# Cross-attention block on one core: inverse roots of the variances on VectorE alone, and the last stage's weights fetched in the last batch

## The reference, cut to what matters

```python
def layer_norm(x, w, b):
    mu = jnp.mean(x, axis=-1, keepdims=True)
    var = jnp.mean(jnp.square(x - mu), axis=-1, keepdims=True)
    return (x - mu) * jax.lax.rsqrt(var + EPS) * w + b

residual = hidden_states
x = layer_norm(hidden_states, ln1_w, ln1_b)
q = x @ q_w + q_b;  k = ctx @ k_w + k_b;  v = ctx @ v_w + v_b      # per head
scores = einsum('bhqd,bhkd->bhqk', q, k) * scale                   # masked
out = einsum('bhqk,bhkd->bhqd', softmax(scores), v)
hidden = out @ cproj_w + cproj_b + residual
y = layer_norm(hidden, ln2_w, ln2_b)
y = gelu(y @ fc_w + fc_b, approximate=True) @ proj_w + proj_b
return hidden + y
```

## Time and profile before

| what | value |
|---|---|
| median of three runs | 750.32 us (749.85 to 750.52) |
| the profiled execution's own time | 747.24 us |
| its span in the trace | 745.4 us |
| TensorE matmuls busy | 698.3 us, 94% of the span |
| ScalarE busy | 457.9 us, 61%; 400.6 of it the 416 exponentials |
| VectorE busy | 370.6 us, 50% |
| GpSimd busy | 122.8 us, 16% |
| mean granted clock of TensorE | 0.981 of full speed |

### The profile page before, as it was taken

How to read it: one execution, slowest core, us unless ns; L and a number is a source line. 1 busy time by engine, 2 the same in 40 slices (tenths; PEclk the granted TensorE clock), 3 DMA queues, 4 the chain that set the end, 5 groups by cost and what they waited for, 6 DMA issues and landing times.

```text
span 745.4 us, 16779 instructions
## 1 busy us (share of the span) xinstructions
PE 698.3 (94%) x7026; PEld 476.8 (64%) x7026; DVE 370.6 (50%) x824; ACT 457.9 (61%) x483; POOL 122.8 (16%) x90
## 2 busy tenths in 40 slices
PE   3679998999999999999999999999998978999997
PEld 3567665666566656665666566656664534697897
DVE  5655663554355535543555355525542322467663
ACT  5406568666865686568656865686566888633311
POOL 6222041003200320041003200410000600011010
PEclk9869999999999999999999999999999999999999
DMA  9677564356544653465346534654435500000000
GB/s 312 185 268 274 185 207 183 136 174 210 189 139 171 210 198 136 165 210 201 137 160 212 199 143 156 211 199 143 160 141 182 187 2 2 1 22 7 30 29 32
DMA packets 51081, 113.76 MB, mean 153 GB/s; under 512 B 6858, under 2 KB 39986, under 8 KB 49722
## 3 DMA queue, kind: packets, MB, share of 16 engines
q1 hardware_dynamic: 40488, 80.56, 31.9%
q10 hardware_dynamic: 10514, 32.08, 11.9%
HBM read 65.30 MB, written 47.06 MB: 151 GB/s over the span
## 4 chain that ended last, share of the span: by engine, by line
PE 77%; ACT 13%; issue 1%; DVE 1%; ACTq 0%; DVEq 0%
PE O L1152 22%; PE S L1145 16%; ACT pr L602 12%; PE XB L1082 11%; PE O L1082 10%; PE O L1239 6%; PE S L1082 6%; PE XB L1179 2%; PE MB L1132 2%; PE XB L1119 2%; PE XB L1111 0%; ACT pj_raw L610 0%; ACT L602 0%; PE O L1132 0%; DVE g_lo L921 0%
## 5 line engine op out<-in xcount | busy, mean ns | idle before, releaser
L602 ACT ACTIVATE pr<-S 128x1024 f32<-128x1024 f32 x416 | 400.6, 1024 | 176.6 <-PE S L1145 172.9
L1152 PE MATMUL O<-pr,vsl 128*17 128x256 f32 x3328 | 224.8, 384 | 1.3 <-DVE ot L816 1.3
L1145 PEld LDWEIGHTS S<-qst,kst 64*128 64x128 f32 x1664 | 116.0, 186 | 117.4 <-ACT pr L602 79.1
L1145 PE MATMUL S<-qst,kst 64*128 64x256 f32 x1664 | 170.5, 313 | 16.9 <-ACT pr L602 13.5
L1152 PEld LDWEIGHTS O<-pr,vsl 128*17 128x17 f32 x3328 | 74.9, 97 | 78.2 <-issue 16.4
L751 DVE TENSOR_SCALAR kpart<-O,cols_s 128x384 fp32r<-128x384 f32 x64 | 40.6, 635 | 120.4 <-PE O L1082 120.4
L526 POOL CAST c_hi<-cT 128x768 fp32r<-128x768 f32 (+1 forms) x28 | 23.9, 852 | 328.4 <-DMA cT<-in_ctx_t 202.9
L797 DVE TENSOR_REDUCE mx<-MB 128x2 fp32r<-128x512 f32 x64 | 44.1, 689 | 64.7 <-PE MB L1132 64.7
L1082 PE MATMUL XB<-w_hi,c_hi 128*128 128x256 f32 (+1 forms) x208 | 68.3, 328 | 2.6 <-DVE vsl L765 1.8
L765 DVE TENSOR_TENSOR vsl<-XB,rows_s 128x256 f32<-128x256 f32 (+1 forms) x104 | 43.3, 416 | 51.0 <-PE XB L1082 51.0
L1082 PE MATMUL O<-c_hi,w_hi 128*128 128x384 f32 (+1 forms) x128 | 52.8, 412 | 17.0 <-POOL c_lo L531 10.5
(11 more groups left out here) (101 smaller groups left out, 842.5 us busy)
## 6 DMA issues: line engine op xcount, KB each, us to landing
kst<-k_scr SPq DMA_DIRECT2D x89, 400.2 KB
k_scr<-kpart SPq DMA_DIRECT2D x48, 384.0 KB, 3.3
v_scr<-vsl ACTq DMA_DIRECT2D x8, 1768.0 KB, 6.0
cT<-in_ctx_t ACTq DMA_DIRECT2D x21, 384.0 KB, 5.0
k_scr<-kpart SPq DMA_DIRECT2D x16, 449.0 KB, 3.3
qst<-q_scr SPq DMA_DIRECT2D x87, 64.0 KB
q_scr<-qpart SPq DMA_DIRECT2D x16, 256.0 KB, 2.5
cT<-in_ctx_t ACTq DMA_DIRECT2D x7, 449.0 KB, 3.5
```

Source lines behind the costliest of these rows:

```text
L602: nc.scalar.activation(pr[:, n % PBUF, :], S[:, 2 * (n % 2):2 * (n % 2) + 2, :] .rearrange("p a n -> p (a n)"), ACT.Exp).then_inc(s_.exp_d ...
L1145: last = nc.tensor.matmul(S[:, 2 * (n % 2) + g_, j * LQ:(j + 1) * LQ], kst[rows_, s, j, kt * P:(kt + 1) * P], qst[rows_, s, j, :], start=T ...
L1152: last = nc.tensor.matmul(O[32 * h:32 * h + VW, 0, 0:LQ], vsl[:, par, s, kt, h * VW:(h + 1) * VW], pr[:, n % PBUF, h * LQ:(h + 1) * LQ], s ...
```

## The change

`newton` becomes `inverse_root`: the first guess comes from the variance's bits, shifted right by one and taken from a constant, and three Newton rounds follow, all on VectorE: eleven instructions, each waiting for the one before. `x_root`, `h_root` and their semaphores go. The five instructions stood at the same places. `load_mlp` moves from step 44 of batch 6 to step 4 of batch 7; its waits are the same. The counts of `ln_steps` and `rstd_steps` follow.

```diff
+ROOT_BITS = 0x5F375A86
+ROUNDS = 3
+NEWTON = 2 + 3 * ROUNDS
...
-            def x_root(t0, t1, steps):
-                act.wait_ge(ln_steps, steps)
-                nc.scalar.activation(rs1[:, 1, t0:t1], rs1[:, 0, t0:t1], ACT.Sqrt).then_inc(ln_root, 1)
-
-            def h_root(s_, i, t0, t1):
-                act.wait_ge(s_.var_done, i + 1)
-                nc.scalar.activation(rs[:, 1, t0:t1], rs[:, 0, t0:t1], ACT.Sqrt).then_inc(s_.root_done, 1)
...
-                    if c == 0 and s_ is first:
-                        h_root(first, 1, HEAD, TOK)
...
-            x_root(0, 2 * QT, XA_VAR)
...
-                    if n == 44 and b + 2 == B:
+                    if n == 4 and b + 1 == B:
                         load_mlp()
-                    if b == 0 and n == 40:
-                        x_root(2 * QT, TOK, XB_VAR)
-                    if b == B - 1 and n == 20:
-                        h_root(first, 0, 0, HEAD)
...
-            def newton(rs_, steps, before, root, roots):
-
-                dve.wait_ge(root, roots)
-                nc.vector.reciprocal(rs_[2], rs_[1]).then_inc(steps, 1)
+            def inverse_root(rs_, steps, before):
+
+                nc.vector.tensor_scalar(rs_[1].bitcast(I32), rs_[0].bitcast(I32), 1, None, ALU.arith_shift_right).then_inc(steps, 1)
                 dve.wait_ge(steps, before + 1)
...
+                nc.vector.tensor_scalar(rs_[2].bitcast(I32), rs_[1].bitcast(I32), -1, ROOT_BITS, ALU.mult, ALU.add
+                                        ).then_inc(steps, 1)
+                for i in range(ROUNDS):
+                    n = before + 2 + 3 * i
+                    dve.wait_ge(steps, n)
+                    nc.vector.scalar_tensor_tensor(out=rs_[3], in0=rs_[2], scalar=-0.5, in1=rs_[2], op0=ALU.mult, op1=ALU.mult
+                                                   ).then_inc(steps, 1)
+                    dve.wait_ge(steps, n + 1)
+                    nc.vector.tensor_tensor(rs_[3], rs_[3], rs_[0], ALU.mult).then_inc(steps, 1)
+                    dve.wait_ge(steps, n + 2)
+                    nc.vector.scalar_tensor_tensor(out=rs_[2], in0=rs_[3], scalar=1.5, in1=rs_[2], op0=ALU.add, op1=ALU.mult
+                                                   ).then_inc(steps, 1)
+                dve.wait_ge(steps, before + NEWTON)
...
                         if s_ is first and c == 1 and i == 0:
-                            newton(rs_rows(rs, HEAD, TOK), first.rstd_steps, TOK + 5, first.root_done, 2)
+                            dve.wait_ge(first.var_done, 2)
+                            inverse_root(rs_rows(rs, HEAD, TOK), first.rstd_steps, TOK + NEWTON)
```

More of the change, by code:

```diff
@@ L277, in build @@
         hi_done, lo_done, kh_done, qh_done, ql_done = map(sem, ("hi_done", "lo_done", "kh_done", "qh_done", "ql_done"))
-        ln_steps, ln_root = sem("ln_steps"), sem("ln_root")
+        ln_steps = sem("ln_steps")
         good_steps, good_ready, flag_done = map(sem, ("good_steps", "good_ready", "flag_done"))
@@ L302, in section @@
             s.var_done = sem(f"{name}_var_done")
-            s.root_done = sem(f"{name}_root_done")
             s.rstd_steps = sem(f"{name}_rstd_steps")
@@ L329, in build @@
         XA_VAR = 4 * QT + 1
-        XB0 = XA_VAR + 5
+        XB0 = XA_VAR + NEWTON
         XB_VAR = XB0 + 2 * (TOK - 2 * QT) + 1
@@ L687, in _ @@
                         exponential(whole, b, n)
-                h_root(whole, 0, 0, TOK)
                 y_t(whole, 0)
@@ L900, in ending @@
                     dve.wait_ge(first.h_steps, ONE + B)
-                    moments(first, HEAD, TOK, HEAD + 5)
+                    moments(first, HEAD, TOK, HEAD + NEWTON)
             def checked():
@@ L958, in _ @@
             head(1)
-            newton(rs_rows(rs1, 0, 2 * QT), ln_steps, XA_VAR, ln_root, 1)
+            dve.wait_ge(ln_steps, XA_VAR)
+            inverse_root(rs_rows(rs1, 0, 2 * QT), ln_steps, XA_VAR)
             k_evac(0, 0, 2)
@@ L1009, in norms @@
                 if b == 0 and p == 24:
-                    newton(rs_rows(rs1, 2 * QT, TOK), ln_steps, XB_VAR, ln_root, 2)
+                    dve.wait_ge(ln_steps, XB_VAR)
+                    inverse_root(rs_rows(rs1, 2 * QT, TOK), ln_steps, XB_VAR)
                 if b == B - 1 and p == 5:
@@ L1014, in norms @@
                 if b == B - 1 and p == 12:
-                    newton(rs_rows(rs, 0, HEAD), first.rstd_steps, HEAD, first.root_done, 1)
+                    dve.wait_ge(first.var_done, 1)
+                    inverse_root(rs_rows(rs, 0, HEAD), first.rstd_steps, HEAD)
                 if b == B - 1 and p == YN_AT:
@@ L1070, in _ @@
                 moments(whole, 0, TOK, 0)
-                newton(rs_rows(rs, 0, TOK), whole.rstd_steps, TOK, whole.root_done, 1)
+                dve.wait_ge(whole.var_done, 1)
+                inverse_root(rs_rows(rs, 0, TOK), whole.rstd_steps, TOK)
                 normalise(whole, 0)
```

8 lines of the change are left out of this document (removed).

## The result

| | before | after |
|---|---|---|
| median, first comparison | 750.09 us (4 runs, 749.58 to 750.52) | 739.14 us (4 runs, 738.16 to 739.85) |
| ratio | | 0.9863 (95%: 0.9837 to 0.9888) |
| median over the later series (the changed kernel with the four above) | 748.85 us (89 runs; 748.87 with the four above) | 739.38 us (14 runs) |
| profiled execution, its span | 747.24, 745.4 us | 738.16, 736.4 us |
| busy: TensorE, ScalarE, VectorE | 698.3, 457.9, 370.6 us | 690.8, 446.9, 379.8 us |

The change makes the kernel 9.5 us faster (748.85 − 739.38). The kernel before also spreads: single executions of it took 745.9 to 755.6 us, so three runs did not give its median to a microsecond.

What follows compares the result with a forecast made beforehand. TensorE, with 77% of the chain, was taken as the bound, waiting on ScalarE's exponentials or VectorE's evacuations. Terms −3.6 − 3.7 − 1.7 + 0.9 + 0.7 = −7.4 us from 750.3 gave 742.9; range 741.2 to 746.8.

Steps and rivals of the forecast that it cites:

- Fetch out of batch 6: Batch 6, pairs 20 to 25: ScalarE no longer waits before exponential 44 to issue the weights' fetch; gain 3.6 us.
- Root out of the last batch: Last batch, between exponentials 19 and 20: load, Sqrt and load leave ScalarE; gain 3.7 us (2.8 to 3.8).
- the first: First batch, before exponential 40: the square root and its pair of table loads leave ScalarE; gain 1.7 us.
- Last stage: Second group of the last stage: eleven VectorE instructions for five make g_lo late; loss 0.7 us (0.3 to 1.2).
- The head: Head: eleven VectorE instructions delay chunk 2's k_evac, TensorE passes it on; loss 0.9 us. Own rival: 2.5 more, chance 0.08.
- The base: Whole kernel: starting time 750.3 us, median of three runs, 3.1 above the profiled execution, a distance assumed to stay.
- GpSimd against VectorE: Last batch, pairs 8 to 11: GpSimd's weight subtractions block VectorE, so maxima come late; costs 2.5 us, 745.4; chance 0.17.
- Weights too late: Last batch: late-fetched weights hold VectorE's normalise or ScalarE's y; slower than before, 752 us or more; chance 0.03.

Runs made afterwards that it cites:

- headroot: Kernel before with the new inverse root in the head alone; median 746.66 us, ratio 0.9981.
- headsqrt: Changed kernel with the old Sqrt and five instructions back in its head; median 739.03 us, 739.65 over both series.
- again: Kernel before, unaltered, measured once more; median 748.94 us, ratio 1.0006.
- loadtwice: Changed kernel with a one-element Sqrt on ScalarE right ahead of exponential 0, so two table loads lie there; median 741.75 us, ratio 0.9906.
- expearly: Kernel before with a one-element exponential after ScalarE's last context load of the head, so the table loads earlier, not ahead of exponential 0; 747.62 us.
- fetch: Kernel before with only the last stage's weight fetch moved from the end of batch 6 to step 4 of the last batch; 744.76 us, ratio 0.9955.
- batchroots: Kernel before with the new inverse root in the first and last batch only; median 743.76 us, ratio 0.9941.
- loadback2: Second measurement of the changed kernel with a one-element Sqrt on idle ScalarE, bringing back the table load ahead of exponential 0; 740.81 us, ratio 0.9891.
- delay12: Kernel before, Sqrt kept, with twelve idle VectorE instructions on 4 columns added behind the head's five; median 751.96 us, ratio 1.0050.

## Why the prediction was right and where it failed

- **Fetch out of batch 6** (−3.6): right, −3.36 at its place, −3.4 alone. Comparing two equal stretches of TensorE, one with and one without the stall, gave it.
- **Root out of the last batch** (−3.7) and **the first** (−1.7): right, −3.7 and −1.7 at their places; alone together −4.4 in the total, whose interval ends at −5.6 and holds the sum −5.4. The 3.7 exceeded ScalarE's own 2.8, as the rows at the lower clock said. By the Trainium skill (ScalarE: Activation LUTs, What ACT_TABLE_LOAD costs), 2.66 us for each switch, two switches would have given an estimated 5.3 us; the stretch gave back 3.7, so the measurement decides against the drain.
- **Last stage** (+0.7): right in size, +0.9 at its place (+0.6 between the means of all profiles with the new and with the old root there), and by g_lo. The waits were spread otherwise: gelu 5 waits 1.66 us, not the 2.4 of the forecast, and gelu 3 already 1.78. Moved one column earlier the root costs nothing there in three profiles of four.
- **The head** (+0.9) is the step that failed. The prediction wrote that TensorE "passes the whole 0.9 on", and of the load before exponential 0 "VectorE's first evacuations hold TensorE there, so I cost it at 0". Measured: headroot −1.4 (−2.6 to −0.1) in the kernel before, and in the changed kernel −0.3 against headsqrt (14 and 12 runs, standard error 0.4). Two things were wrong. First, the load was put at 0 because VectorE was to hold TensorE there. In the changed kernel's profile TensorE's first scores start at 56.04 us and ScalarE, held by its DMA issues until 58.05, is the late one already; a load behind them holds TensorE further. TensorE is busy for 0.50 of the 3 us from 59 to 62 in again, 1.37 in headsqrt, 0.21 in loadtwice, and for 2.42 in the changed kernel, 2.38 in headroot and 2.21 in expearly. That is so where TensorE came at the higher clock; before, fetch, batchroots and loadback2 have the load and are busy for 2.52 to 2.77, at the clock of 0.50 before it. In the total the cost is 2.4 us for two loads and 2.0 for one; expearly points the same way. Second, VectorE's lateness was to be passed on whole. K chunk 2 is emptied at 21.99 us in headroot and at 19.41 in expearly, neither with a load, and transpose 1 comes at 80.05 and 80.20, the medians are 746.66 and 747.62: 2.6 us of lateness cost nothing. The other profiles agree: the q store is issued at 32.0 to 32.4 us in seven of the 20 profiles and at 32.4 to 34.6 in the others, and the first fetch of K behind it starts at 36.77 us on average in the seven and at 36.96 in the others. The prediction argued along one chain, and the fetch waits for others too; which of them decides was not tested.
- **The base** was 1.5 us too high: three runs with the median 750.32 stood for a kernel whose median is 748.85, and "a shorter kernel keeps that distance" of 3.1 us to the profiled one had nothing in the trace behind it. The changed kernel's profiled execution stands 1.2 below its median.
- Together: the terms as predicted sum to −7.4, and 748.85 − 7.4 = 741.4 would have been just in the range. The rest is 2.0 us. The head's miss is 2.3 (from +0.9 to −1.4) by headroot and 1.2 by headsqrt; so it is most of the rest or all of it, and these runs do not say which.
- **Rivals.** GpSimd against VectorE: the mechanism is there in all 11 profiles of the late fetch with the subtractions whole (in ten one VectorE instruction of 3.0 to 4.5 us and no loss), its price in one of them. The same hold in earlier batches, beside c_lo, which the prediction did not list, costs about 1 us far more often. The Trainium skill's rule (SBUF — State Buffer, Who interferes with whom), that the port pair is held for a whole instruction, is what the rows show (4.51 us beside 4.57); TensorE's indifference was to be read only from VectorE's idle time. Weights too late: fc_hi starts 11.4 us after the first issue, not 8.9, which nothing waits for.

**What stays open.** What puts TensorE's clock at one level or the other in 51 to 58 us. Why delay12 is 3.0 us slower than the kernel before, where headroot's lateness cost nothing: its profile, of a quick execution (748.77 us), shows 1.6 of it and belongs to the group with a load at the higher clock, but its other executions have no profile. And whether a load costs the more the later VectorE is: no run here separates that from chance.

## What to carry to other kernels

A table load, or any fixed piece of work on an engine, is free only where its engine has slack when the load runs. "Another engine holds it up there" must be read from a row (who is released last), and from more than one profile where executions differ, above all at the start of a pipeline, where the engine has just come from issuing DMAs. Where a wait is taken away early in a kernel, list what now starts earlier on the other engines: here GpSimd's unbroken subtractions cost VectorE 1.3 us. And measure the spread of the kernel before: a base from three runs can be off by more than a term.

## What the hardware showed that I had not expected

- VectorE's instruction on 128x4 elements (the variances, L726 after) took 1.50 us beside GpSimd's 128x768 subtraction and 0.17 in its gap; in 11 of the 12 profiles with the new head it took 1.48 to 1.79. The same on 128x14 took 0.25 to 1.88 us in the 14 profiles with the late fetch and 0.17 to 0.18 in the six others. It reads one tensor and no second.
- Between two GpSimd subtractions back to back VectorE sometimes gets one instruction through (att 0.28 us at 597.55 beside pj_lo at 597.53) and sometimes not (4.73 us at 599.73). In four pieces of 128x512 the subtractions took 5.00 us instead of 4.57, and no VectorE instruction beside them more than 1.15.
- An integer shift, an integer multiply and add and the two-operation forms on 128x2 to 128x14 follow one another, each waiting for the one before, every 0.20 to 0.21 us.
- The same program reached transpose 1 at 79.84, 80.02 and 82.59 us in three executions, with the granted clock of 44 to 58 us at 0.63, 1.00 and 0.72.
